# GpSimd's waits for its gathers, at every fourth (sixth) gather and between chunks, in a four-layer graph network

## The reference

```python
x = x + _L0_gnn_ref(h, edge_index, ...)                   # two attention layers
    e = leaky_relu(alpha_s[src] + alpha_d[dst], SLOPE)
    p = jnp.exp(e - segment_max(e, dst)[dst])
    out = segment_sum(h[src] * (p / z[dst])[:, :, None], dst)
x = x + _L1_gnn_ref(h, ..., edge_index, edge_type_8)      # two relation layers
    msg = sum over r of where(edge_type == r, x[src] @ W[r])
    agg = segment_sum(msg * norm[:, None], dst)
x = x + _L2_gnn_ref(...)                                  # sheaf layer
x = x + _L3_gnn_ref(h, edge_attr_16, ..., edge_type_90)   # 90 types
    msg = einsum('ei,eio->eo', h[src], W_rel[edge_type]) * e
```

## Time and profile before

| | us |
|---|---|
| median of 3 runs | 25891.91 |
| lowest and highest run | 25857.63, 25914.94 |
| span of the profiled execution | 25860.5 |
| PE busy in it | 20502.8 (79%) |
| DVE busy in it | 19538.6 (76%) |
| POOL busy in it | 14550.5 (56%) |

### The profile page before, as it was taken

The page is one execution under the profiler, slowest core; times in us unless marked ns, Lnnn a source line. Parts: engine busy times, 40 slices in busy tenths (PEclk is TensorE's granted clock), DMA queues, the critical chain, the costliest instruction groups (busy, mean ns, idle before and its releaser), DMA issues. The chain is left out here.

```text
span 25860.5 us, 355868 instructions
## 1 busy us (share of the span) xinstructions
PE 20502.8 (79%) x110397; PEld 18592.4 (72%) x110397; DVE 19538.6 (76%) x36629; ACT 12983.1 (50%) x15054; POOL 14550.5 (56%) x14357
## 2 busy tenths in 40 slices
PE   0688874888885799978999638888888889489996
PEld 0577763888785688867888538888888888278885
DVE  4699995777776699987999626666666667499997
ACT  0455551222221466644666316666666667266664
POOL 1555545555554555554555467666776675355555
PEclk9999996999997899998999859999999999599998
DMA  5222221111111111111111111111111111522221
GB/s 91 59 71 71 71 69 22 37 40 37 40 37 31 37 40 40 40 32 40 36 35 35 23 14 19 19 19 18 19 18 19 19 19 15 147 67 71 71 71 50
DMA packets 1347467, 1106.63 MB, mean 43 GB/s; under 512 B 937658, under 2 KB 1197972, under 8 KB 1320180
## 3 DMA queue, kind: packets, MB, share of 16 engines
q1 hardware_dynamic: 673364, 571.63, 8.0%
q0 software_dynamic: 545440, 167.01, 7.8%
q10 hardware_dynamic: 127872, 358.35, 3.8%
HBM read 646.52 MB, written 448.94 MB: 42 GB/s over the span
## 5 line engine op out<-in xcount | busy, mean ns | idle before, releaser
L973 PE MATMUL gat_e_found<-gat_e_parts,gat_e_lowhot 128*128 128x400 f32 x27776 | 5657.0, 363 | 1270.4 <-DVE gat_e_rows L937 974.6
L973 PEld LDWEIGHTS gat_e_found<-gat_e_parts,gat_e_lowhot 128*128 128x128 f32 x27776 | 5301.1, 199 | 1625.9 <-DVE gat_e_rows L937 1225.8
L1091 POOL DMA_INDIRECT gat_e_rows<-att_t,gat_e_index x3968 | 3767.0, 949 | 3046.1 <-issue 1509.8
L1966 PEld LDWEIGHTS rgcn_e_found<-rgcn_e_parts,rgcn_e_lowhot 128*128 128x128 f32 x23808 | 4295.3, 188 | 667.9 <-DVE rgcn_e_picked L1811 455.5
L760 POOL DMA_INDIRECT rgcn_e_rows<-rel_t,rgcn_e_index x3472 | 3284.4, 946 | 2506.3 <-DMA rgcn_e_rows<-rel_t,rgcn_e_index 1137.9
L1966 PE MATMUL rgcn_e_found<-rgcn_e_parts,rgcn_e_lowhot 128*128 128x400 f32 x23808 | 4543.8, 348 | 173.4 <-DVE rgcn_e_picked L1811 133.8
L2527 PE MATMUL sheaf_e_bysrc<-sheaf_e_exacthot,sheaf_e_masked 128*128 128x392 f32 x19840 | 4217.8, 370 | 423.7 <-ACT sheaf_e_exacthot L2630 365.4
L2258 POOL DMA_INDIRECT sheaf_e_rows<-sheaf_t,sheaf_e_index x3224 | 3386.3, 1050 | 1695.5 <-issue 886.8
L2527 PEld LDWEIGHTS sheaf_e_bysrc<-sheaf_e_exacthot,sheaf_e_masked 128*128 128x128 f32 x19840 | 3844.2, 206 | 533.1 <-ACT sheaf_e_exacthot L2630 400.0
L2630 ACT CAST sheaf_e_exacthot<-sheaf_e_eighthhot 128x1568 fp32r<-128x1568 bf16 x2480 | 3587.9, 1501 | 919.9 <-DVE sheaf_e_eighthhot L2341 549.4
L973 PE MATMUL typed_e_found<-typed_e_parts,typed_e_lowhot 128*128 128x400 f32 x11904 | 2372.3, 351 | 338.0 <-DVE typed_e_hrows L937 242.1
(11 more groups left out here) (515 smaller groups left out, 27971.4 us busy)
## 6 DMA issues: line engine op xcount, KB each, us to landing
rgcn_e_low<-few_low_d SPq DMA_DIRECT2D x124, 768.0 KB
typed_e_types<-in_type_t SPq DMA_DIRECT2D x62, 1536.0 KB
sumsatt<-gat_e_sums ACTq DMA_DIRECT2D x62, 1404.0 KB
typed_t<-typed_p_y SPq DMA_DIRECT2D x98, 765.0 KB
sumsatt<-gat_e_sums ACTq DMA_DIRECT2D x62, 1092.0 KB
gat_e_rows<-att_t,gat_e_index POOLq DMA_INDIRECT x3968
rgcn_e_rows<-rel_t,rgcn_e_index POOLq DMA_INDIRECT x3472
sumsrel<-rgcn_e_sums ACTq DMA_DIRECT2D x124, 416.0 KB
```

Source lines behind the costliest of these rows:

```text
L973: last = pe.matmul(self.found_ps[n % 2][:, c + b, 0:w], hot[:, k, col * P:(col + 1) * P], self.table.column(part, k)[:, b * w:(b + 1) * w] ...
L1091: pool.indirect_dma_start(rows_t[a.k][:, j, :], None, table, rows(index[a.k][:, j:j + 1]))\
L1966: last = pe.matmul(found_ps[c // 2][:, c % 2, 0:FHI * FD], low_hot[at % 2][:, n, c * P:(c + 1) * P], short.column(part, n), start=n == 0 a ...
```

## The change

`DRAIN` goes from 6 to 4 and `LONG_DRAIN` from 9 to 6: GpSimd waits before gathers 4, 8, 12, 16, 20 and 24 of a chunk of 28, and before 6, 12, 18, 24 and 30 of a chunk of 36. A new function `drain_before` makes it wait, before it begins a chunk, until all gathers of the chunk before have landed.

```diff
-DRAIN = 6
-LONG_DRAIN = 9
+DRAIN = 4
+LONG_DRAIN = 6
...
+def drain_before(pool, g, gathered, turn, k, cols):
+
+    pool.wait_ge(gathered[1 - k], turn * (16 * cols) + k * (16 * cols))
+    pool.sem_inc(g.gate, 1)
...
-    def gather_chunk(self, pool, g, table, turn, k):
-
+    def gather_chunk(self, pool, g, table, turn, k, first=False):
+
+        if not first:
+            drain_before(pool, g, self.gathered, turn, k, self.cols)
         self.wait_to_gather(pool, turn, k)
         pool.sem_inc(g.gate, 1)
         for j in range(self.cols):
...
     def gather(self, pool, g, table):
         for k in range(2):
-            self.gather_chunk(pool, g, table, 0, k)
+            self.gather_chunk(pool, g, table, 0, k, first=k == 0)
...
                 def gather(a, fresh=False):
+                    if not (fresh and a.k == 0):
+                        drain_before(pool, g, gathered, a.turn, a.k, JG)
                     if not fresh:
                         pool.wait_ge(rows_used, a.c - 1)
```

## The result

| | us |
|---|---|
| kernel before, median of 4 runs | 25885.59 (25857.63 to 25914.94) |
| changed kernel, median of 4 runs | 26323.97 (26314.72 to 26337.61) |
| ratio, 95% interval | 1.0172 (1.0159 to 1.0185) |
| span of the profiled execution | 26335.9, before 25860.5 |

The change costs 438 us. Slower was right, the size was not.

A forecast was written before the change was run, and what follows sets the result against it. POOL was taken to work through each pass beside DVE with little left over, so added stops make DVE wait: +258, +198, +215 and +77 sum to +748 us, giving 26640 us, range 26340 to 26960.

The forecast's parts named there:

- The limits in the four passes: Average stop POOL can bear before being late: 2.104 us first attention, 1.842 and 1.803 relation, 2.423 typed.
- the lead: How early POOL's last gather lands before DVE wants it, spent once a pass: 26.6 to 38.7 us.
- least in the typed pass, and there only late: DVE's waits for gathers were to be smallest in the typed pass and start late there.
- The price of a stop: Average POOL wait for landings, floor about 2.2 us: 2.7 first attention, 2.3 relation, 2.6 us typed pass.
- the surplus of before: Stop time above the floor in first attention pass, from bursts of other transfers: 3.6 us a chunk, spread over seven stops.
- rival 2: Stops meet loads starting at the same landing, doubling the burst surplus in the four passes: +1134 us (27030), 10%.
- The second attention pass costs nothing: Its added stops, 3.8 us a chunk plus one between chunks, fit inside POOL's 11.4 us wait for DVE.
- 7.6 us remain in each chunk: POOL's wait for DVE in the second attention pass left over after its two added stops.
- rival 4: PE idles more and its granted clock falls; at 0.85, 180 us more in each relation pass: 27000, 4%.
- rival 1: Stops replace time POOL would idle anyway, so no change (25892); not slower 4%, actually faster 2%.
- rival 3: All stops at the 2.2 us floor, bursts harmless: +369 us, nothing in the typed pass (26260), 7%.

The follow-up runs named there:

- e12: Changed kernel with the typed pass loading one column of `types` instead of 24 in its loop; +1093 us against the kernel before, ratio 1.0455.
- first pair: The original measurement of the kernel before and the changed kernel, chip not on record: medians 25885.59 and 26323.97 us.
- later runs: The follow-up experiments on three chips, each compared with the kernel before on its own chip, which takes 24.00 to 24.03 ms there.
- e5: The whole change run once more against the kernel before on the same chip; +1236 us, ratio 1.0512.
- e4: The whole change except in the second attention pass, against the kernel before; +913 us, ratio 1.0380.
- e9: Kernel before with the opening matmul issued three times instead of once in the second attention pass; +485 us against the kernel before, ratio 1.0203.
- e10: Changed kernel with the opening matmul issued three times in the second attention pass; +1400 us against the kernel before, ratio 1.0583.
- e13: Kernel before with ten copies of both opening matmuls in three found tiles per second-attention chunk; +472 us against the kernel before, ratio 1.0196.
- e14: Changed kernel with ten copies of both opening matmuls in three found tiles per second-attention chunk; +1372 us against the kernel before, ratio 1.0571.
- e7: Kernel before with only the stop between chunks added in all five passes, DRAIN = 6 and LONG_DRAIN = 9; +228 us, ratio 1.0094.
- e11: Kernel before with DRAIN = 14 and LONG_DRAIN = 18, one stop in each chunk; -76 us, ratio 0.9968.

## Why the prediction was right or wrong

- **The limits in the four passes: right.** The idle time of before, plus the lead, over 433 stops gave 1.80 to 2.42 us as what POOL can bear. Measured stops in these limits give +704 of time, and the sum closes to 12 us. (The stops are taken from the idle time after, so what this tests is that POOL sets the passes and that the leads are spent.) DVE's waits for gathers were not spread as I said, though: "least in the typed pass, and there only late" is wrong, with 150.3 us in 51 waits against 143.6 in the first relation pass. The lead is gone at the end of each pass; the changed kernel's last gather of the typed pass and DVE behind it, to be held against the earlier trace rows:

```profile
26157.84 0.94 POOL L3043 DMA_INDIRECT typed_e_rows<-typed_t,typed_e_index  x1 [0.30 <-issue]
26160.32 0.21 DVE L3087 TENSOR_TENSOR typed_e_weight<-typed_e_weight,typed_e_dst 128x52 f32<-128x52 f32 x1 [12.23 <-DMA typed_e_rows<-typed_t,typed_e_index]
```

- **The price of a stop: three sizes off, nearly cancelling.** First attention pass 2.47, not 2.7 (+160 in place of +258): I had spread the surplus of before, 3.6 us a chunk, over seven stops, but only 7 x 0.27 = 1.9 us of it came back. Before, the stop before gather 18 took 4.94 us on average; after, the longest are those before gathers 20 and 24, with 2.96 and 2.89. Nor did more stops find a burst more often. Relation passes 2.26 and 2.24, not 2.3 (+183 and +190 for +198 and +215). Typed pass 2.82, not 2.6 (+171 for +77): rival 2's locking, which I had priced at 2.9 there, is real in this pass, and of the four only in it; e12 shows the load that does it.
- **"The second attention pass costs nothing": the step that failed.** It gave 258 us back in the first pair, which is nearly the whole miss of 310. "7.6 us remain in each chunk" was a right reading of the earlier trace rows for the first pair: without its waits for DVE, POOL needed 50.7 us a chunk before and 58.2 after, still less than the 61.7 that the pass took. But the pass did not keep its length. I took POOL's wait for DVE as room, and did not ask why DVE was late there: no engine is busy for over 52 of 62 us a chunk, so something held PE and DVE up that no sum of mine contained. In the later runs this room is absent and the same edit costs 363. Nor had I a rival in which this pass moved by itself, to either side.
- **What stays open.** Why that pass is slow in the first pair (and the sheaf pass too, 6669 to 5864 us), and why the change made it less so. The traces do show where the time goes. One place in the trace of before, PE, then DVE:

```profile
5022.14 11.96 PE L973 MATMUL gat_e_found<-gat_e_parts,gat_e_lowhot 128*128 128x400 f32 x64 [1.55 <-issue]
5037.45 7.85 PE L973 MATMUL gat_e_found<-gat_e_parts,gat_e_lowhot 128*128 128x400 f32 x33 [3.35 <-DVE gat_e_rows L937]
```

```profile
5035.38 0.99 DVE L930 TENSOR_TENSOR gat_e_picked<-gat_e_found,gat_e_highhot 128x800 f32<-128x800 f32 x1 [3.86 <-PE gat_e_found L973]
```

  The 64 matmuls are four found tiles of 16. Counted from the begin of the pass, the tile that DVE starts on at 5035.38 is the third of them, and its last matmul ended at 5031.19 (ends of matmuls are modelled by the profile). So DVE stood for 3.86 us although its tile was done, and PE then stood for DVE.

  The same count over the whole pass, wherever DVE stood for more than 0.3 us at L930, gives how long before its start the tile's last matmul had ended: 2.8 us in the median before (362 times), 1.2 us after (268 times), and 0.04 us in e5 (107 times), which is the same program as after. From DVE's read to PE's next matmul it is 0.06 us in all three. In the sheaf pass DVE starts 2.9 us (median) after the last matmul into `sheaf_e_vp` in both traces of the first pair, and 0.04 us after it in e4 and e5.

  What is late in these two passes of the first pair is thus the step from PE to DVE. What delays it, and why the changed kernel's second attention pass has less of it, no run shows. The imitations (e9, e10, e13, e14) slowed PE itself, not this step, and didn't bring the gain out; the later runs never were as slow as the first pair, so its cause is untested.
- **The other rivals.** The clock (rival 4) fell as it said, but not far: 0.96 to 0.92 in the first attention pass and 1.00 to 0.97 in the first relation pass (granted clock over the pass), above the 0.90 below which PE would be the bound in the relation pass. "Nothing changes" (rival 1) had its mechanism, room that hides stops, in parts of later runs only: the second attention pass of e10 and e14 against e9 and e13, and the first relation and typed pass of e7. Stops at the floor everywhere (rival 3, 26260) is near the measured time by accident: its stops are too short in the first attention and the typed pass, and it has no gain in the second.
- **The Trainium skill against the trace.** Counted from the end of the gather's time on POOL, as I did, the stops held: the shortest average of a pass is 2.24 us. By the 2.0 us that the Trainium skill, "DMA: Bandwidth & Descriptors", section "Anatomy of one DMA — SWDGE (gpsimd) path", has for a whole small DMA, counted from the gather's begin, there would have been no cost, and there was.

## What to carry to other kernels

Idle time of an engine is room only once you can name what it waits for and why that is late; if no engine is near its limit in the stretch, as here, the room may be absent in the next trace. A cost per chunk is best judged as a limit, idle time plus lead over the number of stops, and then by what a stop costs beside the loads that start on the same landing. Two kinds of stops share one room: each alone can look cheap.

## What the runs showed of the hardware

- The same program ran in 25.89 ms in the first pair and, on three chips, in 24.00 to 24.03 ms in the later runs. In the changed kernel, four passes paced by POOL's gathers differed by 0.3% or less between the first pair and e5, the second attention pass by 2.1%; the unchanged sheaf pass by 14% (6669 and 5864 us).
- In the second attention and the sheaf pass of the first pair DVE started 1.2 to 2.9 us (medians) after the end of the matmuls that it waited for, in e5 0.04 us. The other way, from DVE to PE, took 0.06 us in both (second attention pass).
- DVE goes on sooner after a landing than POOL. The last gather of the typed pass ends on POOL at 26158.78 and DVE starts at 26160.32, 1.54 us later, 2.48 us after the gather's begin; in the five passes of the changed kernel it is 2.32 to 2.48 us after the begin. POOL itself goes on 2.2 us after the end of a gather that it waited for, 2.0 at the least.
- With up to 14 or 18 gathers in flight in place of 6 or 9 (e11) a gather on POOL still takes 0.944 to 0.957 us, and the stop 2.19 to 2.34 us on average, 2.66 in the second attention pass.
- Beside a load of 1536 KB that starts on the same landing a stop took 5.2 us, without it 2.4 (e5 and e12).
